# Starting the adjacency gathers beside the loads of x in a two-layer graph attention kernel

## The chip, the cores and the metric

One Trainium2 chip, one core. The metric is the device time of one execution in microseconds (us), as the median of several runs. A profile, taken by the hardware profiler on one execution, gives the times of single instructions and transfers, counted from the start of its span.

## What is computed

Two graph attention layers with residuals on 8192 nodes of 128 features; the adjacency is an 8192 x 8192 int32 matrix, 268 MB, and both layers read it.

```python
h = relu(layernorm(x)); x = x + L0(h, adj)      # L0: attention, threshold 1e-4, times row degree, elu
h = relu(layernorm(x)); x = x + L1(h, adj)      # L1: attention
# in each layer
h = input @ W
e = leaky_relu((h @ a_src)[:, None] + (h @ a_dst)[None, :], 0.2)
att = softmax(where(adj > 0, e, NEG), axis=1)
out = att @ h
```

## The kernel before

The kernel replaces the softmax by a form in which a weight is a maximum of two products, one factor for the row and one for the column, times the adjacency's 0 or 1. For each layer `sum_tiles` runs over 8 groups of 1024 rows and in each over 64 tiles of 128 columns: VectorE forms a weight tile of 128 x 1024 (L906), TensorE multiplies it with h in eight matmuls of 128 x 129 (L659). That is 16384 matmuls in all.

The adjacency comes in by pieces. `load_piece` (GpSimd, L328) gathers 128 rows of 1024 int32 by an indirect DMA, with the row numbers from the tile `piece_rows`; `mask_piece` (ScalarE, L337) turns one into bytes; `turn_edges` (VectorE, L355) transposes the bytes of eight tiles at a time. A pass has 32 pieces (`PIECES`); there are 31 passes, 992 pieces. There are six buffers for pieces (`NA`): gather n, from n = 6 on, waits until mask n - 5 is done. The buffers that the gathers write are not those of x.

The work that comes first is the projection of layer 0. x (8192 x 128 f32, 4.2 MB) is loaded in 8 parts (`XP`) of 1024 rows, each by four DMAs of 128 KB with rows of 512 B: two of each part from SP's queue, two from ScalarE's (`load_x`, L398). SP's queue also has the weights of layer 0 ahead of x and those of layer 1 between parts 3 and 4 (L441 to L445). In the DMA views SP's queue is q1, ScalarE's q10, and that of GpSimd's gathers q0.

Every engine has its order written out by hand, and waits on semaphores in that order. On VectorE (L938 to L980): statistics of parts 0 to 3 (L715), their variance, statistics of part 4, `inverse` for the first half, normalising of parts 0 and 1 (L740), statistics of parts 5 to 7, variance of the second half, normalising of parts 2 and 3, the second inverse, and then `keep_h` (L761), `keep_zT` (L756) and normalising in turn, `extreme_values` with `lin` (L791), `diagonals`. On TensorE (L677 to L691): `turn_z` (L621) for part i + 1 ahead of `products` (L632) for part i, then `spread`, then the sums. On ScalarE (L555 to L568): its 16 loads of x, the square root for the first half (`deviation`, L495), then the 32 masks of the first pass, with `keep_first_zT` 0 to 3 (L504) ahead of masks 3, 4, 7 and 8, the second square root ahead of mask 6, and the exponentials of layer 0 (`exps`, L545 to L552) ahead of mask 30.

On GpSimd (`pool_fast`, L367) `ident` and the first row numbers are made (four IOTAs, L379), then all 992 gathers are issued one after the other. Ahead of the first gather GpSimd waits for part 3 of x, which with the parts before it is half of x, and ahead of the fourth gather for part 7, the last. After gather 48 it makes the other row numbers (eight IOTAs).

Of the kernel before, what the change touches and what calls it, by code (L numbers as in the profile page):

```python
# [44 lines left out]
XP = 8  # L45
# [9 lines left out]
BK = 4  # L55
# [25 lines left out]
def kernel_program(nc, x, adj, W0, a0, W1, a1, out):  # L81
# [10 lines left out]
    def sem(name):  # L92
        if name not in sems:
            sems[name] = ctx.enter_context(nc.semaphore(name))
        return sems[name]

    with ctx:
# [107 lines left out]
        x_loaded = [sem(p + f"x_loaded{i}") for i in range(XP)]  # L205
# [122 lines left out]
        def load_piece(pool, n):  # L328
            g, c, h, k, a = piece(n)
            if n >= NA:  # L330
                pool.wait_ge(masked, n - NA + 1)
            column = ((g * G + 2 * k + h) * BK + a) * COLS + c
            pool.indirect_dma_start(adj_in[n % NA], None, adj_pieces,  # L333
                                    bass.IndirectOffsetOnAxis(ap=piece_rows[:, column:column + 1], axis=0))\
                .then_inc(adj_in_loaded[n % NA], 16)
# [31 lines left out]
        def pool_fast(pool):  # L367
            steps = [0]

            def step(ins):  # L370
                steps[0] += 1
                ins.then_inc(index_made, 1)
                pool.wait_ge(index_made, steps[0])

            def indices(c, t0, t1):
                for b in range(BK):
                    q = slice(b * BP, (b + 1) * BP)
                    tt = slice((c * CT + t0) * BK * COLS, (c * CT + t1) * BK * COLS)
                    step(nc.gpsimd.iota(piece_rows[q, tt].rearrange("p (t a c) -> p t a c", a=BK, c=COLS),  # L379
                                        pattern=[[BP * (N // LC), t1 - t0], [N // LC * LC, BK], [BK, COLS]],  # L380
                                        base=b + (c * CT * P + t0 * BP) * (N // LC), channel_multiplier=N // LC))

            nc.gpsimd.memset(ident[:], 0.0).then_inc(ident_made, 1)
            pool.wait_ge(ident_made, 1)
            nc.gpsimd.affine_select(out=ident[:], in_=ident[:], compare_op=ALU.not_equal, fill=1.0,
                                    base=0, pattern=[[-1, P]], channel_multiplier=1).then_inc(ident_made, 1)
            pool.wait_ge(ident_made, 2)
            indices(0, 0, G)
            pool.wait_ge(x_loaded[XP // 2 - 1], 16 * BK)
            for n in range(len(PASSES) * PIECES):  # L390
                load_piece(pool, n)
                if n == 2:
                    pool.wait_ge(x_loaded[XP - 1], 16 * BK)
                if n == PIECES + PIECES // 2:
                    indices(0, G, CT)
                    indices(1, 0, CT)
# [636 lines left out]
        def fast_program():  # L1033
            with nc.Block() as block:
                @block.sync
                def _(sp):
                    sync_fast(sp)

                @block.scalar
                def _(act):  # L1040
                    scalar_fast(act)

                @block.tensor
                def _(pe):
                    tensor_fast(pe)

                @block.vector
                def _(dve):
                    vector_fast(dve)

                @block.gpsimd
                def _(pool):
                    pool_fast(pool)
# [645 lines left out]
```

## Time and profile before

| | |
|---|---|
| median of 3 runs | 2001.0 us (1999.59 to 2002.02) |
| profiled execution | 2002.71 us, of which its span is 2000.9 us |
| TensorE busy | 1914.1 us, 96% of the span |
| VectorE, ScalarE, GpSimd busy | 87%, 73%, 63% |
| HBM read and written | 548.54 MB and 16.32 MB |

The profiled execution lies 1.7 us above the median. Times inside it are from the start of the span. An engine's busy time says how much it works, not whether it is late; for that, read the chain of work that ended last, and the waits.

### The profile page before, as it was taken

How to read it: one execution, taken by the hardware profiler on the slowest of the kernel's cores; microseconds unless marked ns; L12 is line 12 of the kernel's file. 1: busy time of each engine (PE TensorE's matmuls, PEld its weight loads, DVE VectorE, ACT ScalarE, POOL GpSimd, SP SyncE). 2: the span in 40 equal slices, each digit the busy share in tenths (PEclk: the TensorE clock that was granted, in tenths of full speed). 3: DMA queues.
4: the chain of work that ended last, by engine and by line, in shares of the span. 5: the costliest groups of instructions: out<-in, count | busy, mean ns of one | idle time of the engine just before them, and what ended most of it. 6: DMA issues, size and time to landing. Idle time of an engine off the chain costs nothing.

```text
span 2000.9 us, 39030 instructions
## 1 busy us (share of the span) xinstructions
PE 1914.1 (96%) x16858; PEld 1902.6 (95%) x16858; DVE 1750.4 (87%) x2026; ACT 1453.3 (73%) x1677; POOL 1255.5 (63%) x1010
## 2 busy tenths in 40 slices
PE   4789999999999999999968999999999999999997
PEld 3689999999999999999967999999999999999997
DVE  7888898989989898998957998898989899898985
ACT  4988788969888798888820767777777777778700
POOL 3675766767777676767720556767777776768600
PEclk9799999999999999999988999999999999999999
DMA  8998897999989898897982777888988888889900
GB/s 247 350 339 340 287 334 245 335 335 317 317 287 320 275 321 304 280 320 272 325 283 96 269 295 275 293 311 293 337 276 325 283 296 309 294 315 306 316 10 13
DMA packets 182339, 567.49 MB, mean 284 GB/s; under 512 B 18704, under 2 KB 50832, under 8 KB 180752
## 3 DMA queue, kind: packets, MB, share of 16 engines
q0 software_dynamic: 142848, 520.16, 74.4%
q1 hardware_dynamic: 34960, 42.67, 6.4%
q10 hardware_dynamic: 4352, 2.10, 0.5%
q8 instruction: 133, 2.18, 0.4%
q14 instruction: 46, 0.38, 0.1%
HBM read 548.54 MB, written 16.32 MB: 282 GB/s over the span
## 4 chain that ended last, share of the span: by engine, by line
PE 89%; DVE 6%; DMA 2%; ACT 1%; POOL 1%; issue 0%; SPq 0%; DVEq 0%; POOLq 0%
PE psum L659 87%; PE psum L632 1%; DMA arena<-in_adj_dram,piece_rows 1%; DVE arena L906 1%; DVE arena L740 1%; DVE arena L891 1%; ACT arena L343 1%; DVE arena L884 1%; PE psum L621 0%; DMA arena<-in_x_dram 0%; DVE st L715 0%; POOL piece_rows L379 0%; PE psum L599 0%; DVE arena L361 0%; DVE h_all L761 0%
## 5 line engine op out<-in xcount | busy, mean ns | idle before, releaser
L659 PE MATMUL psum<-h_all,arena 128*128 128x129 f32 x16384 | 1842.4, 276 | 10.4 <-DVE arena L906 10.4
L659 PEld LDWEIGHTS psum<-h_all,arena 128*128 128x128 f32 x16384 | 1837.9, 192 | 14.0 <-DVE arena L906 9.2
L333 POOL DMA_INDIRECT arena<-in_adj_dram,piece_rows x992 | 1246.1, 1256 | 641.4 <-ACT arena L343 446.1
L343 ACT ACTIVATE arena<-arena,half_step 128x1024 uint8<-128x1024 int32 x992 | 1365.1, 1437 | 313.1 <-DVE arena L361 161.3
L906 DVE SCALAR_TENSOR_TENSOR arena<-arena,rho_col 128x1024 f32<-128x1024 f32 x896 | 1125.8, 1277 | 169.1 <-PE psum L659 165.0
L361 DVE STREAM_TRANSPOSE arena<-arena 128x1024 f32<-128x1024 f32 x248 | 305.9, 1234 | 9.1 <-ACT arena L343 9.1
L906 DVE SCALAR_TENSOR_TENSOR arena<-psum,rho_col,arena 128x1024 f32<-128x1024 f32 x128 | 158.7, 1267 | 17.7 <-PE psum L659 14.6
L343 ACT ACTIVATION_READ_ACCUMULATOR arena<-arena,half_step 128x1 f32 x512 | 91.0, 178 | 0.0
L632 PE MATMUL psum<-W_ext,arena 128*128 128x131 f32 x256 | 40.5, 324 | 13.8 <-DVE h_all L761 10.7
L632 PEld LDWEIGHTS psum<-W_ext,arena 128*128 128x128 f32 x256 | 38.1, 234 | 15.4 <-issue 8.1
L621 PE MATMUL psum<-ident,arena 128*128 128x128 f32 x128 | 20.0, 308 | 32.9 <-DVE arena L740 32.5
L621 PEld LDWEIGHTS psum<-ident,arena 128*128 128x128 f32 x128 | 16.9, 160 | 33.9 <-DVE arena L740 33.5
L528 ACT ACTIVATE arena<-arena 128x1024 f32<-128x1024 f32 x8 | 8.5, 1057 | 54.7 <-DVE arena L845 54.7
L740 DVE TENSOR_SCALAR arena<-arena,mean,rstd 128x128 f32<-128x128 f32 x128 | 35.2, 365 | 0.1
L508 ACT ACTIVATE arena<-psum 128x1024 f32<-128x1024 f32 x8 | 8.2, 1024 | 32.3 <-PE psum L621 32.2
L715 DVE BATCH_NORM_STATS2 st<-arena 128x6 f32<-128x128 f32 x128 | 26.0, 277 | 2.5 <-DMA arena<-in_x_dram 2.4
L517 ACT ACTIVATE sd_next<-psum 128x12 f32<-128x12 f32 x16 | 2.9, 181 | 24.7 <-PE psum L632 24.7
L827 DVE TENSOR_TENSOR h_all<-h_all,D_col 128x1024 f32<-128x1024 f32 x16 | 19.4, 1215 | 0.0
L538 ACT ACTIVATE arena<-h_all,invalid 128x128 f32<-128x128 f32 x64 | 19.4, 386 | 0.0
L845 DVE SCALAR_TENSOR_TENSOR arena<-psum,inv,arena 128x128 f32<-128x128 f32 x64 | 17.8, 342 | 0.0
L884 DVE SCALAR_TENSOR_TENSOR arena<-mean_row,fl,arena 128x128 f32<-128x128 f32 x64 | 17.5, 348 | 0.3
L891 DVE SCALAR_TENSOR_TENSOR arena<-psum,inv,arena 128x128 f32<-128x128 f32 x64 | 17.3, 343 | 0.3
(111 smaller groups left out, 180.9 us busy)
## 6 DMA issues: line engine op xcount, KB each, us to landing
arena<-in_adj_dram,piece_rows POOLq DMA_INDIRECT x992, 5.9
arena<-in_x_dram SPq DMA_DIRECT2D x48, 128.0 KB, 6.2
x_mid<-arena SPq DMA_DIRECT2D x8, 512.0 KB, 5.5
edgesT<-arena SPq DMA_DIRECT2D x4, 1024.0 KB, 8.9
arena<-edgesT SPq DMA_DIRECT2D x4, 1024.0 KB, 11.1
arena<-r_mid SPq DMA_DIRECT2D x1, 4096.0 KB, 12.0
arena<-x_mid SPq DMA_DIRECT2D x8, 512.0 KB, 6.8
out_dram<-arena SPq DMA_DIRECT2D x32, 128.0 KB, 9.8
```

Source lines behind the costliest of these rows:

```text
L333: pool.indirect_dma_start(adj_in[n % NA], None, adj_pieces, bass.IndirectOffsetOnAxis(ap=piece_rows[:, column:column + 1], axis=0))\
L343: nc.scalar.activation(pack_bytes[h][:, k, a], adj_in[n % NA], ACT.Sign, bias=half_step[:, 0:1], accum_out=into).then_inc(masked, 1)
L361: nc.vector.transpose(edge_words[:, slot(at), h], pack_words[h][:, s * SBT:(s + 1) * SBT])\
L538: last = nc.scalar.activation(tiles(hr)[:, t, :], h_all[:, b, 0:F], ACT.Identity, scale=D_inv[:, b:b + 1])
L621: last = nc.tensor.transpose(zT_ps(layer, i)[:, t * P:(t + 1) * P], z[:, t, :], ident[:])
L632: last = nc.tensor.matmul(h_ps(layer, i, half)[:, t, :], zT[:, b * P:(b + 1) * P], W_exts[layer][:, 0:HZ], start=True, stop=True)
L659: last = nc.tensor.matmul(acc_tile(g, k), wTs[m % RING][:, k * P:(k + 1) * P], h_all[:, j, 0:FZ], start=(j == 0 and k % 2 == 0), stop=(j = ...
L715: last = nc.vector.bn_stats(st[:, i * TP + t, :], source[:, t, :])
L740: last = nc.vector.tensor_scalar(into[:, t, :], source[:, t, :], mean[:, b:b + 1], rstd[:, b:b + 1], ALU.subtract, ALU.mult)
L884: last = nc.vector.scalar_tensor_tensor(xr[:, cols], mean_row[:], fl[:, k:k + 1], xr[:, cols], ALU.mult, ALU.add)
L891: last = nc.vector.scalar_tensor_tensor(xo[:, cols], acc_tile(g, k)[:, 0:F], inv[:, k:k + 1], xr[:, cols], ALU.mult, ALU.add)
L906: nc.vector.scalar_tensor_tensor(wTs[m % RING].rearrange("p (k n) -> p k n", k=BK), r_of(layer, g), rho_col[:, j:j + 1], edge_bytes[:, slo ...
```

## The change

The two waits of GpSimd for x are taken out. Its gathers are issued as soon as their row numbers stand, six of them, and from the seventh on as each mask frees a buffer.

```diff
             indices(0, 0, G)
-            pool.wait_ge(x_loaded[XP // 2 - 1], 16 * BK)
             for n in range(len(PASSES) * PIECES):
                 load_piece(pool, n)
-                if n == 2:
-                    pool.wait_ge(x_loaded[XP - 1], 16 * BK)
                 if n == PIECES + PIECES // 2:
                     indices(0, G, CT)
                     indices(1, 0, CT)
```

## Rows read from the trace of the kernel before

**Rows 1.** The page, parts 1 and 2: busy us; busy tenths in 40 slices.
```profile
PE 1914.1 (96%) x16858; PEld 1902.6 (95%) x16858; DVE 1750.4 (87%) x2026; ACT 1453.3 (73%) x1677; POOL 1255.5 (63%) x1010
...
PE   4789999999999999999968999999999999999997
```

**Rows 2.** Windows: stretch, its length, busy us (instructions) of each engine, clock, DMA share, GB/s.
```profile
120.00:137.50 17.50, 11.44 (x103) 11.25 (x102) 9.09 (x9) 17.10 (x25) 11.92 (x13) 0.92 1.02 404
137.50:1000.00 862.50, 862.50 (x7707) 862.50 (x7708) 790.05 (x898) 727.78 (x1056) 609.07 (x473) 1.00 0.89 308
```

**Rows 3.** The chain of work, 0 to 160 us: start us, us, what.
```profile
9.15 8.32 DMA arena<-in_x_dram
...
17.50 1.65 DVE st L715 x8
...
37.95 3.85 PE psum L632 x16
...
75.61 0.18 DVE lin L791
...
137.50 22.58 PE psum L659 x183
```

**Rows 4.** Waits of VectorE up to 45 us, of ScalarE up to 80: total, times, longest.
```profile
DVE st L715 <- DMA arena<-in_x_dram: 2.4, 4, 0.7
...
ACT std L495 <- DVE var L725: 5.7, 1, 5.7
...
ACT r_col L545 <- DVE lin L791: 1.3, 1, 1.3
```

**Rows 5.** Timeline: start us, us, engine, line, operation [idle before it and its releaser].
```profile
1.55 1.55 POOL L379 IOTA piece_rows<- 32x64 int32 x4
...
14.78 1.12 POOL L333 DMA_INDIRECT arena<-in_adj_dram,piece_rows  x1 [11.67 <-DMA arena<-in_x_dram]
...
16.20 0.94 POOL L333 DMA_INDIRECT arena<-in_adj_dram,piece_rows  x1 [0.30 <-issue]
...
22.50 0.94 POOL L333 DMA_INDIRECT arena<-in_adj_dram,piece_rows  x1 [4.11 <-DMA arena<-in_x_dram]
...
23.39 1.45 ACT L343 ACTIVATE arena<-arena,half_step 128x1024 uint8<-128x1024 int32 x1 [6.35 <-DMA arena<-in_adj_dram,piece_rows]
...
43.09 1.02 ACT L504 ACTIVATE arena<-psum 128x1024 f32<-128x1024 f32 x1 [4.26 <-PE psum L621]
...
45.56 1.95 PE L632 MATMUL psum<-W_ext,arena 128*128 128x131 f32 x16
```

**Rows 6.** DMA, 5 to 12 us (packets, MB, share of 16 engines); windows, 12 to 19.
```profile
DMA packets 3988, 1.93 MB, mean 275 GB/s; under 512 B 229, under 2 KB 3988, under 8 KB 3988
...
12.00:19.00 7.00, 0.00 (x0) 0.00 (x0) 5.65 (x31) 0.23 (x1) 3.00 (x3) 1.00 1.25 220
```

**Rows 7.** DMA, 22 to 24.5 us.
```profile
q0 software_dynamic: 269, 0.98, 102.6%
```

**Rows 8.** DMA, 96 to 103 us.
```profile
q0 software_dynamic: 599, 2.16, 85.3%
q1 hardware_dynamic: 661, 0.35, 17.5%
```

**Rows 9.** Landing of the loads L427 (80 to 100 us), and of L400 (0 to 10).
```profile
DMA to landing us min/median/max: 11.8/15.0/16.4
...
DMA to landing us min/median/max: 3.0/6.2/9.5
```

**Rows 10.** Landing of the first gather, issued at 14.78 us.
```profile
DMA to landing us min/median/max: 8.6/8.6/8.6
```

**Rows 11.** DMA, 18 to 22 us.
```profile
q1 hardware_dynamic: 726, 0.35, 60.1%
q0 software_dynamic: 142, 0.54, 53.0%
```

**Rows 12.** Windows, as in rows 2.
```profile
38.00:39.00 1.00, 1.00 (x5) 1.00 (x6) 0.42 (x1) 0.83 (x2) 0.00 (x0) 0.50 0.59 86
```

## The prediction

> **What bounds the kernel now.** I read the page first. TensorE is busy for 1914.1 of 2000.9 us, VectorE for 87% of the span, ScalarE for 73%, GpSimd for 63% [rows 1]; in the slices TensorE's digit is 9 all the way except in the first four and at the layer boundary. So the end is set by when TensorE's long run starts. The windows say when that is: from 137.50 to 1000 us TensorE is busy for 862.50 of 862.50 us, and between 120 and 137.5 it works 11.44 us of 17.5 [rows 2]. Whatever moves the restart at 137.5 us moves the end one for one; whatever lies ahead of it and doesn't move it costs nothing.
>
> Then I followed the chain of work back from that restart. It goes through transfers of the adjacency, the mask on ScalarE, an IOTA on GpSimd, to masks that stand behind the exponentials, and these behind VectorE's `lin` at 75.61 us. From there back it is VectorE (statistics, normalising, keeping h) with products on TensorE between, to the statistics at 17.50 us, and these are released by a load of x issued at 9.15 us that took 8.32 us [rows 3]. What isn't in the chain ahead of `lin` is to be seen too: no gather and no mask. The start is a chain of x.
>
> The waits up to 80 us say how near the others are. VectorE waits four times for x, 2.4 us in all. ScalarE waits 5.7 us for the variance and 1.3 us for `lin` [rows 4], 6.35 us for its first gather and 4.26 us for TensorE's fourth transpose [rows 5]. So ScalarE is never the late one ahead of the exponentials.
>
> **What the change removes.** GpSimd's two waits. The first gather is issued at 14.78 us after 11.67 us of waiting for x, the fourth at 22.50 us after 4.11 us [rows 5]. The four IOTAs end at 1.55 + 1.55 = 3.10 us, so the first gather now goes out at about 3.4 us. Issues are 1.24 us apart (16.20 to 17.45), so six of them, as many as there are buffers, are issued by 3.4 + 6 x 1.24 = 10.8 us. The seventh waits for the first mask, as before. No instruction is added; the number of gathers is unchanged.
>
> **What that gives.** The first mask ran at 23.39 us. Now it is held by the code ahead of it on ScalarE, the square root at 16.81 us, so it could run at 17.1 us: 6.3 us earlier. But the eighth mask is followed by `keep_first_zT(3)`, which waits for TensorE's transpose, which waits for VectorE; it ran at 43.09 us after 4.26 us of idling [rows 5]. Masks that are earlier only lengthen that idling. Gain: 0. Behind 43.09 us nothing is different, since six buffers are full then in either kernel; and even there ScalarE had 1.3 us left before `lin`. Bounds: 0 and 0.
>
> **What it costs.** Gathers now share the 16 DMA engines with x. A piece is 128 x 1024 int32, 0.524 MB; six are 3.15 MB. With x alone (5 to 12 us) the two queues move 3988 packets in 7 us, 570 per us, of 512 B: 275 GB/s with the engines busy throughout, about 1.0 MB on each queue [rows 6]. So x has no idle engines to give away. Gathers alone (22 to 24.5 us) move 0.98 MB in 2.5 us, 392 GB/s [rows 7]. When both have work (96 to 103 us, the loads of `load_xr`, of 512 B rows too, beside gathers) the gather queue has 599 packets and SP's queue 661: one for one by packets, which by bytes is 2.16 MB against 0.35 [rows 8]. Those four loads took 11.8 to 16.4 us to land, x at the start 3.0 to 9.5 [rows 9].
>
> Now the sum. 661 small packets at 570 per us are 1.2 us, so 599 gather packets cost 5.8 us, 103 per us. The six gathers need 599 x 3.15 / 2.16 = 873 packets. With three queues in turn a round costs 1/103 + 2/570 us, 75 rounds per us: 11.6 us until the gathers are through, in which x gets 1746 packets, worth 3.1 us of its own time. x falls behind by 8.5 us. From bytes, 3.15 MB at 392 GB/s, it is 8.0 us. I take 7.5 us, since with x alone the rate sagged to 220 GB/s over 12 to 19 us [rows 6], in which a gather finds some room.
>
> Is all of it ahead of the load that counts? That is part 4 of x: issued at 9.15 us, in use at 17.50. Before, no gather had been issued until part 3 had landed. The first gather landed 8.6 us after its issue [rows 10], of which its own 0.524 MB take 1.3 us at 392 GB/s, so a first packet may lag its issue by anything up to 7.3 us. From 3.4 us that is 3.4 to 10.7 us, and 11.6 us later, at 15 to 22 us, the six are done. Part 4 would land near 25 us, behind them in either case. Part 3 is late by nearly the same.
>
> What is late next: VectorE's statistics at 17.50 us go to 25, and with them the inverse, the normalising, every `keep_h`, `lin`, the exponentials, masks 30 and up, and the restart. On VectorE all is in order behind the wait; TensorE and ScalarE wait for VectorE. The slack on the way: 0.7 us ahead of the statistics, but that is itself a wait for x, so none. Parts 5 to 7 are wanted only after parts 0 and 1 are normalised, and have 8 us of x's stream behind part 4 to come in; they cost nothing more. Nothing between 17.5 and 137.5 us in the chain starts by a time of its own, so the delay is passed on whole. Bounds of the cost: 0 (the gathers find no turn before x is through) and 14.6 us. The latter goes by 18 to 22 us, when the mix had 0.35 + 0.54 MB in 4 us, 222 GB/s [rows 11]: with x's share as in rows 8, 3.15 MB of gathers carry 0.51 MB of x along, 3.66 MB are 16.5 us, less 1.9 us that x's part takes alone. I stay by rows 8, since there both queues have work for all of 7 us, at 2.51 MB or 359 GB/s, while 18 to 22 us holds the gathers' first packets only.
>
> The Trainium skill, page "DMA: Bandwidth & Descriptors", section "Queues, rings and completion order", has each engine take one packet from each queue that has work, in turn; by that gathers get their turn as soon as they are there, which speaks against the change and against rival 1. Rows 8 agree, rows 11 at first sight don't. The same page, "Specifications", puts the limit from HBM at about 358 GB/s for a core; rows 7 show 392, so the measurement decides; by the page's figure the six gathers would cost 8.8 us in place of 8.0.
>
> **Forecast.** Sum against the profiled execution: 2002.7 (span 2000.9 and 1.8 around it) + 7.5 = 2010.2 us. The median of the runs, 2001.0, lies 1.7 under that execution, so I predict 2001.0 + 7.5 = 2008.5 us.
>
> **Rival 1: x goes first anyway, no change.** In the row of 18 to 22 us, SP's queue moved 726 packets and the gathers 142, though the first gather had been issued at 14.78 [rows 11]. If gathers get in only as x drains, part 4 lands at 17.5 to 18.5 us and the delay is 0 to 1 us: 2001.5 us. For it: the 8.6 us landing. Against it: one for one in rows 8, and that the end of x's queue is what 18 to 22 us shows. A partial form (gathers start late, three of six ahead of part 4) gives 3 to 4 us: 2004.5. Chance of a delay under 4 us, both forms: 0.25.
>
> **Rival 2: faster, by TensorE's clock.** Three groups of 16 products lie in the chain ahead of `lin`, the first at 37.95 us with 3.85 us [rows 3], while the same 16 take 1.95 us at 45.56 us [rows 5]; the clock granted at 38 us was 0.50, 1.2 GHz [rows 12]. Masks that come earlier let ScalarE do `keep_first_zT(0)` as soon as TensorE has turned part 0, ahead of when it did, and with it TensorE's first products, which shifts TensorE's activity. If x isn't late and all three groups come into stretches at 2.4 GHz, 3 x 1.9 = 5.7 us go: 1995.3 us. It decides the sign only if x is late by less than 5.7 us. Against it: VectorE sets when these groups start, and the pauses between them stay. Chance of faster: 0.08.
>
> **Rival 3: the mix is worse than steady.** If small and large packets together hold the engines to rates between those of rows 8 and rows 11, x is 9.5 to 14.6 us late; the middle gives 2001.0 + 12 = 2013.0 us. For it: the start has three queues at once, rows 8 only two. Against it: rows 8 ran at 359 GB/s for 7 us. Chance 0.12.
>
> **Numbers.** What 3 to 5 runs can tell from no change is about 0.2%, 4 us. Forecast with its near cases (4 to 9.5 us late) 0.55, rival 3 0.12: slower 0.67. Delay or gain under 4 us: 0.25. Faster 0.08. The range takes in rival 1 and the nearer half of rival 3, 2000.5 to 2012.5; the forecast's own is 2005.5 to 2010.5.
>
> **What would show it.** GpSimd's first gather at 3.4 us with no wait for x. VectorE's statistics of part 4 at about 25 us instead of 17.50, and its waits for x near 10 us in place of 2.4. In the DMA rows of 8 to 16 us three queues with nearly equal packets, about 75 per us each. First mask at about 24.5 us, held by the square root. `keep_first_zT(3)` at about 50.5 us. `lin` at 83 us and TensorE's restart at 145 us. The prediction is wrong if the statistics of part 4 stay near 17.5 us, or if they are late but the restart isn't: then ScalarE's masks, not x, had carried the chain.

## The result, and the profile after

The changed kernel takes 2007.33 us (median of 8 runs, 2005.78 to 2011.16) against 2000.39 us (8 runs, 1996.10 to 2002.59): a ratio of 1.0041, 95% interval 1.0029 to 1.0053, so 6 to 11 us slower (6.9 by the two medians). Forecast were 2008.5 us and 7.5 us more. The profiled execution has a span of 2009.3 us, 8.4 us over that of before.

The timeline of the changed kernel, start us, us, engine, line, operation, with the idle time before it and its releaser; its answers to [rows 5] and to the statistics of x's parts 1 to 4:

```profile
3.38 1.12 POOL L333 DMA_INDIRECT arena<-in_adj_dram,piece_rows  x1 [0.28 <-POOL piece_rows L379]
...
9.77 0.93 POOL L333 DMA_INDIRECT arena<-in_adj_dram,piece_rows  x1 [0.30 <-issue]
10.47 12.57 SPq L397 DMA_DIRECT2D arena<-in_x_dram  x8
11.89 1.65 DVE L712 BATCH_NORM_STATS2 st<-arena 128x6 f32<-128x128 f32 x8 [2.52 <-DMA arena<-in_x_dram]
17.61 1.65 DVE L712 BATCH_NORM_STATS2 st<-arena 128x6 f32<-128x128 f32 x8 [4.07 <-DMA arena<-in_x_dram]
...
22.52 1.65 DVE L712 BATCH_NORM_STATS2 st<-arena 128x6 f32<-128x128 f32 x8 [3.27 <-DMA arena<-in_x_dram]
...
25.57 1.65 DVE L712 BATCH_NORM_STATS2 st<-arena 128x6 f32<-128x128 f32 x8 [0.15 <-DMA arena<-in_x_dram]
25.58 1.42 ACT L343 ACTIVATE arena<-arena,half_step 128x1024 uint8<-128x1024 int32 x1
...
51.46 1.02 ACT L501 ACTIVATE arena<-psum 128x1024 f32<-128x1024 f32 x1 [4.79 <-PE psum L618]
```

The gathers go out at 3.38 to 9.77 us with no wait for x. VectorE waits for every part of x that comes beside them, and begins part 4 at 25.57 us in place of 17.50. The first mask isn't 6 us earlier but 2 us later (25.58 for 23.39): it stands behind the square root, and that behind x. The wait ahead of `keep_first_zT(3)` is still there, 4.79 us for 4.26.

The chain of work of the changed kernel, the answer to [rows 3], and one window, the answer to [rows 2]:

```profile
12.22 13.32 DMA arena<-in_x_dram
...
25.57 1.65 DVE st L712 x8
...
46.31 3.84 PE psum L629 x16
...
83.80 0.18 DVE lin L788
...
145.43 24.59 PE psum L656 x199
```

```profile
145.43:1000.00 854.57, 854.57 (x7634) 854.57 (x7635) 782.03 (x886) 719.80 (x1050) 592.43 (x469) 1.00 0.88 308
```

Read down the two chains: 8.07 us late at part 4, 8.36 at the products on TensorE, 8.19 at `lin`, 7.93 at the restart, 8.4 at the end. It is the same chain link by link, begun later. Its first link, a load of x in flight, has grown from 8.32 to 13.32 us, and it begins 3.07 us later (12.22 for 9.15 us), since SP takes longer over the issues ahead of it. So of the 8.07 us at part 4, 5.00 are in flight and 3.07 ahead of the issue.

VectorE's waits up to 55 us, the answer to [rows 4], and DMA packets in the changed kernel by queue over 8 to 14 and 14 to 20 us (packets, MB, share of 16 engines):

```profile
DVE st L712 <- DMA arena<-in_x_dram: 10.2, 5, 4.1
```

```profile
q0 software_dynamic: 395, 1.47, 72.3%
q1 hardware_dynamic: 566, 0.27, 17.5%
q10 hardware_dynamic: 526, 0.25, 15.6%
...
q0 software_dynamic: 450, 1.62, 72.6%
q1 hardware_dynamic: 582, 0.28, 17.1%
q10 hardware_dynamic: 576, 0.28, 16.3%
```

By packets each of x's queues has 1.3 to 1.4 times what the gathers have; by bytes the gathers have three quarters. x had 1.93 MB in 7 us before [rows 6]; here both its queues together have 1.08 MB in 12 us. At 8 us ten gather packets had moved, and behind 20 us nine more, so nearly all of the six gathers went by in these 12 us.

### The profile page after: what moved, and what is told of

It is laid out like the page before. It is cut to its first block, busy times and chain, and to the rows that moved or that the text cites. A ratio compares the mean times of both kernels' runs of the same rounds, so it can differ in the third digit from the quotient of the medians.

```text
span 2009.3 us, 39029 instructions
## 1 busy us (share of the span) xinstructions
PE 1914.0 (95%) x16858; PEld 1902.8 (95%) x16858; DVE 1750.0 (87%) x2026; ACT 1454.0 (72%) x1677; POOL 1249.0 (62%) x1010
## 4 chain that ended last, share of the span: by engine, by line
PE 89%; DVE 6%; DMA 2%; ACT 1%; POOL 1%; SPq 1%; issue 0%; DVEq 0%; POOLq 0%
PE psum L656 87%; PE psum L629 1%; DMA arena<-in_adj_dram,piece_rows 1%; DVE arena L903 1%; ACT arena L343 1%; DVE arena L888 1%; DVE arena L737 1%; DVE arena L881 1%; DMA arena<-in_x_dram 1%; PE psum L618 1%; DVE st L712 0%; POOL piece_rows L379 0%; PE psum L596 0%; SPq L397 0%; DVE arena L361 0%
## 5 line engine op out<-in xcount | busy, mean ns | idle before, releaser
L842 DVE SCALAR_TENSOR_TENSOR arena<-psum,inv,arena 128x128 f32<-128x128 f32 x64 | 17.8, 342 | 0.0
```

## The experiments

Theory A: gathers take time of the DMA engines from x, and what reaches the engines ahead of x's part 4 delays everything. Its rivals, in the expectations: any gather beside x is passed on (B), any work in GpSimd's queue costs the same (C), the number of descriptors counts and not their size (D), masks carry the chain (E), gathers' bytes delay x in whatever packets (F). Diffs are against the kernel before, where nothing else is said. The twelve kernels ran in three groups of four, each beside new runs of the kernel before (median 1999.69 us in the first group, 1998.84 in the third). The ratios are those on record with their intervals, and not quotients of the medians, from which they differ by up to 0.0007.

**Which wait pays.** The wait for all of x is taken out, the one for half of x stays.

```diff
             for n in range(len(PASSES) * PIECES):
                 load_piece(pool, n)
-                if n == 2:
-                    pool.wait_ge(x_loaded[XP - 1], 16 * BK)
```

> The wait for half of x is kept, the wait for all of x ahead of the fourth gather is left out. Theory A (gathers take DMA engine time from x, and only what reaches the engines ahead of x's part 4 counts): the first gather goes out at 14.8 us, its first packet near 19, so part 4 is in by 17.5 us as in the kernel before; parts 5 to 7 are late by the three further gathers, up to 4 us, against a slack of about 6 us on VectorE. Statistics of part 4 at 17.5 us, restart of TensorE at 137.5 us, time 2000 to 2001 us, ratio 1.000. Rival B (any gather beside x is passed on to the end, also through parts 5 to 7): 4 us later, ratio 1.002.

Measured: 2000.72 us, ratio 1.0003 (0.9992 to 1.0015). Rival B falls: its 1.002 is outside. Its timeline has all six gathers issued between 14.54 and 20.94 us, the last three of them 4 us earlier than before, and VectorE is not held:

```profile
14.54 1.12 POOL L333 DMA_INDIRECT arena<-in_adj_dram,piece_rows  x1 [11.44 <-DMA arena<-in_x_dram]
...
16.70 1.64 DVE L713 BATCH_NORM_STATS2 st<-arena 128x6 f32<-128x128 f32 x8 [0.16 <-DMA arena<-in_x_dram]
...
20.94 0.94 POOL L333 DMA_INDIRECT arena<-in_adj_dram,piece_rows  x1 [0.30 <-issue]
...
25.26 4.73 DVE L713 BATCH_NORM_STATS2 st<-arena 128x6 f32<-128x128 f32 x24
```

Part 4 is there at 16.70 us and parts 5 to 7 have no wait at 25.26. With the first wait kept, the second is worth nothing. With the first gone it is worth about half of the loss, as the next runs show: it then holds three of the six gathers back.

**How much for how many.** First three gathers early, then one.

```diff
             indices(0, 0, G)
-            pool.wait_ge(x_loaded[XP // 2 - 1], 16 * BK)
             for n in range(len(PASSES) * PIECES):
                 load_piece(pool, n)
                 if n == 2:
                     pool.wait_ge(x_loaded[XP - 1], 16 * BK)
```

> Only the wait for half of x is left out; the wait for all of x ahead of the fourth gather stays, so three gathers (1.57 MB) run beside x. Theory A: half the cost of the changed kernel, 1.57 MB at 392 GB/s = 4.0 us: statistics of part 4 at 21.5 us, restart at 141.5 us, time 2004.4 us, ratio 1.002. Rival C (what costs is that GpSimd's queue has any work ahead of x, say by filling rings, whatever its amount): the full 8 us, ratio 1.004.

```diff
             indices(0, 0, G)
-            pool.wait_ge(x_loaded[XP // 2 - 1], 16 * BK)
             for n in range(len(PASSES) * PIECES):
                 load_piece(pool, n)
+                if n == 0:
+                    pool.wait_ge(x_loaded[XP // 2 - 1], 16 * BK)
                 if n == 2:
```

> One gather goes out at 3.4 us, the next two wait for half of x and the rest for all of x. Theory A: 0.52 MB at 392 GB/s = 1.3 us: statistics of part 4 at 18.8 us, restart at 138.8 us, time 2001.7 us, ratio 1.0007. Rival C: the full 8 us.

Measured: with three, 2004.88 us, ratio 1.0022 (1.0012 to 1.0032); with one, 2002.84 us, 1.0009 (1.0000 to 1.0019). Part 4 in the two timelines, three and one:

```profile
21.92 1.64 DVE L714 BATCH_NORM_STATS2 st<-arena 128x6 f32<-128x128 f32 x8 [0.38 <-DMA arena<-in_x_dram]
```

```profile
18.60 1.65 DVE L716 BATCH_NORM_STATS2 st<-arena 128x6 f32<-128x128 f32 x8
```

| gathers ahead of part 4 | part 4 begins, us | later than before | ratio | TensorE's restart, us (foretold) |
|---|---|---|---|---|
| 0 (before) | 17.50 | | 1 | 137.50 |
| 1 | 18.60 | 1.10 | 1.0009 | 136.72 (138.8) |
| 3 | 21.92 | 4.42 | 1.0022 | 139.75 (141.5) |
| 6 (the change) | 25.57 | 8.07 | 1.0041 | 145.43 (145) |

That is 1.1 to 1.5 us per gather; 0.524 MB at 392 GB/s are 1.34. The cost goes by the amount, so rival C falls.

The restarts with one and three gathers missed what was expected. With one early gather it came 0.78 us earlier than before, with three 2.25 us later in place of 4. TensorE's longest stretch at 1.2 GHz between 64 and 96 us was 20 us long before and after the change, but 14 us in the execution with three and 7 us in that with one. In the latter the chain of work also leaves VectorE at 44.5 us and goes on through ScalarE's masks to the exponentials, and `lin` is only 0.44 us later than before. That the delay reaches the end is shown here by the medians of 12 runs, and for one gather only just.

**Bytes or descriptors.** Six more gathers, of rows an eighth as long, go out at 3.4 us; nobody uses what they bring, and GpSimd waits for them beside half of x.

```diff
+            small = adj.rearrange("r (w n) -> (r w) n", n=P)
+            for i in range(NA):
+                pool.indirect_dma_start(adj_in[i][:, 0:P], None, small,
+                                        bass.IndirectOffsetOnAxis(ap=piece_rows[:, i:i + 1], axis=0))\
+                    .then_inc(small_loaded, 16)
             pool.wait_ge(x_loaded[XP // 2 - 1], 16 * BK)
+            pool.wait_ge(small_loaded, 16 * NA)
```

> The kernel before, with six more gathers of 128 rows of 512 B (in place of 4096 B) ahead of its first wait, which nobody uses; they are in the same number as the early gathers of the change, with as many descriptors, and an eighth of the bytes. GpSimd waits for them together with half of x. Theory A (engine time by bytes): 6 x 128 = 768 packets at 570 per us are 1.3 us: statistics of part 4 at 18.8 us, ratio 1.0007. Rival D (the number of descriptors or turns, or GpSimd's issuing of them, holds x up, whatever their size): 8 us, statistics of part 4 at 25.5 us, ratio 1.004.

Measured: 2000.58 us, ratio 1.0003 (0.9993 to 1.0013). In its timeline the last of them is issued as in the changed kernel, part 4 is 0.35 us late, and GpSimd's own gathers begin at 17.45 us in place of 14.78, behind its second wait:

```profile
9.82 0.94 POOL L392 DMA_INDIRECT arena<-in_adj_dram,piece_rows  x1 [0.30 <-issue]
...
17.85 1.65 DVE L722 BATCH_NORM_STATS2 st<-arena 128x6 f32<-128x128 f32 x8 [0.69 <-DMA arena<-in_x_dram]
```

The same number of gathers, issued at the same times, with an eighth of the bytes costs next to nothing, less than the 1.3 us of theory A. Rival D falls as far as it means the number of gathers or GpSimd's issuing. It doesn't fall by this run as far as it means packets. DMA over 3 to 18 us:

```profile
DMA packets 8127, 3.96 MB, mean 264 GB/s; under 512 B 1070, under 2 KB 8031, under 8 KB 8127
...
q0 software_dynamic: 192, 0.39, 9.8%
```

The small gathers' 0.39 MB went by in 96 packets of 4096 B (8127 less 8031), beside 96 short ones, and not in 768 of 512 B. So the packets became fewer along with the bytes: 192, where the change has 864. Against a cost by the number of packets speak rows of the changed kernel. At x's 570 packets per us 864 would take 1.5 us, and 8 were lost. Over 14 to 20 us 450 gather packets took 72.6% of the engines' time and 582 of x's took 17.1%, so that one held an engine about 5.5 times as long as the other.

**The second four.** These ran on a chip on which the kernel before took 2220.62 us in place of 2000. Their ratios, in the order below, are 1.0095 (1.0047 to 1.0144), 1.0009 (0.9961 to 1.0057), 1.0100 (1.0029 to 1.0172) and 1.0106 (1.0030 to 1.0181). They don't follow x: the third kernel is 1% slower, though its part 4 is earlier (17.01 us, against 17.50 in the kernel before on the first chip). The first, third and fourth lie above what was expected, and why stays open. Only the first 30 us of the profiles are read here; where the kernel was run again, part 4 began within 0.3 us of the same time (17.17 and 17.11 us, 16.34 and 16.08).

The first gather waits for all of x; then layer 1's weights behind x; then x in rows of 4096 B, without and with the change:

```diff
-            pool.wait_ge(x_loaded[XP // 2 - 1], 16 * BK)
+            pool.wait_ge(x_loaded[XP - 1], 16 * BK)
             for n in range(len(PASSES) * PIECES):
                 load_piece(pool, n)
-                if n == 2:
-                    pool.wait_ge(x_loaded[XP - 1], 16 * BK)
```

> The opposite of the change: the first gather waits for all of x (22.5 us in place of 14.8), so nothing runs beside x. It tests the other half of the argument, that ScalarE's early masks have slack. Theory A: the first mask moves from 23.4 to about 27.5 us. The wait ahead of keep_first_zT(3) (4.3 us) takes most of it, but the second square root, ahead of mask 6, comes about 4 us late, at 37.9 us, and VectorE wants it at 35.8: 2 us late there, time 2002 to 2003 us, ratio 1.001; x's part 4 stays at 17.5 us or comes a little earlier. Rival E (masks carry the chain): 4 us and more, ratio 1.002.

```diff
             for i in range(XP):
                 load_x(sp, i, 0)
-                if i == 3:
-                    load_weights(1, W1, a1)
+            load_weights(1, W1, a1)
```

> The kernel before, with the three loads of layer 1's weights moved on SP's queue from between parts 3 and 4 of x to behind part 7. They have 256 packets of 4 B and 128 of 512 B on the queue that part 4 uses. Theory A (x's part 4 carries the start): part 4 lands about 1.5 us sooner, the statistics of part 4 start at 16.8 us right behind the variance in place of 17.5, and the gain is 0.7 us or less: ratio 0.9997 to 1.000, not to be told by the time. If the weights come late for TensorE (wanted at about 23.5 us) that is lost again.

```diff
+        def long_quarters(ap, i):
+            c, u = divmod(i, XP // COLS)
+            four = ap.rearrange("(c b u j t) f -> c b u j t f", c=COLS, b=BK, u=XP // COLS, j=BP)
+            return [(slice(b * BP, (b + 1) * BP), four[c, b, u]) for b in range(BK)]
...
-            for q, block in quarters(x, i)[2 * which:2 * which + 2]:
+            for q, block in long_quarters(x, i)[2 * which:2 * which + 2]:
```

> The kernel before, with x loaded as rows of 4096 B (each partition takes eight neighbouring rows of x) in place of eight rows of 512 B: the same bytes, an eighth of the packets; x's rows go to other partitions than the rest of the kernel takes them for. Theory A: x alone moves near 390 GB/s in place of 275, parts 3 and 4 land earlier, VectorE's statistics run back to back from about 7 us and part 4's are through at about 16 us: 2 to 3 us gained, 1998 us, ratio 0.999.

> The changed kernel with x in rows of 4096 B, as in the run with long rows. Theory A says that the change costs 8 us because in one round of three queues x moves 2 x 512 B beside 4096 B of gather. With rows of one size x has two thirds of the bytes: 2.6 MB up to part 4 need 3.9 MB in all, 10 us from 2.2 us on and about 2 to land, 14 to 15 us. VectorE, bound by its own statistics, is through with part 4 at 17 us or before: the change costs 0 to 2 us here against the kernel with long rows, ratio to the kernel before 0.999 to 1.000. Rival F (gathers' bytes delay x by themselves, in whatever packets): 6 to 8 us against the kernel with long rows.

Read from them: part 4 began at 17.17 us with all of x first, at 16.34 with the weights last, at 17.01 with long rows (14 to 16 had been expected) and at 26.71 with long rows and the change, which nothing had foretold. For the last, here are the packets by queue over 14 to 20 us:

```profile
q0 software_dynamic: 250, 0.90, 58.0%
q10 hardware_dynamic: 230, 0.62, 40.8%
q1 hardware_dynamic: 245, 0.06, 7.3%
```

SP's queue moved 245 packets but 0.06 MB. Between parts 3 and 4 it has layer 1's weights, whose two vectors are 128 packets of 4 B each. By these counts such a packet takes a turn like any other, while the two other queues move up to 4096 B in theirs. The four were run again, the two with long rows now with the weights behind part 7; part 4 then began at 14.61 us in place of 17.01, and at 19.23 in place of 26.71.

**The third four.** All of x first:

> The opposite of the change once more: the first gather waits for all of x. Theory A: first mask at about 26.7 us, second square root at 37.5 and VectorE's second inverse at 37.8 us in place of 35.8; 2 us late from there, ratio 1.001. Rival E (masks carry the chain): 4 us and more, ratio 1.002.

Measured: 2002.34 us, ratio 1.0013 (1.0004 to 1.0022). VectorE's second inverse is 2.15 us later than before (35.84), released by the square root, as expected; but TensorE's products, 3.83 us long before, are short in this execution:

```profile
37.99 0.35 DVE L728 RECIPROCAL rstd<-std 128x32 f32<-128x32 f32 x1 [2.34 <-ACT std L493]
...
40.16 2.02 PE L630 MATMUL psum<-W_ext,arena 128*128 128x131 f32 x16 [1.77 <-DVE h_all L759]
```

The granted clock over 35 to 45 us was 1.00, against 0.66 in the kernel before. TensorE's first products came later there (32.86 us for 28.58), and with less time ahead of the second (3.4 us for 5.6); I take that for the reason, but no run shows it alone. It more than made the loss of 2 us good in the profiled execution (`lin` 2.1 us earlier than before), and not in the median. The ratio is nearer to A's 1.001 than to rival E's 1.002, whose value the interval reaches. The wait for the square root has the size that A gave it. But the chain of work of this execution doesn't go through VectorE:

```profile
22.36 1.12 POOL arena L333
...
44.11 30.22 ACT arena L343 x44
74.33 0.15 ACT r_col L543
```

It goes from the first gather through ScalarE's masks to the exponentials, which ScalarE reached 0.8 us behind `lin`. So with all of x first the masks did carry the chain in this execution, as rival E says, though not at its price; E isn't excluded by this run. Gathers can be issued too late as well, but 7.6 us later (22.36 us) cost only 2.6 us by the ratio (0.8 to 4.4).

Weights of layer 1 last:

> The kernel before with layer 1's weights behind part 7 of x, once more. Theory A: statistics of part 4 at 16.3 to 16.8 us in place of 17.5, the second inverse about 1 us earlier than 35.8, ratio 0.9995, not to be told from 1 by the time.

Measured: 2000.74 us, ratio 1.0008 (0.9999 to 1.0018). The trace went a little further than foretold, with part 4 at 16.08 us, the second inverse at 34.36 and `lin` at 74.15, 1.5 us earlier than before; the time didn't follow. Inconclusive, and no gain.

Long rows with the weights last, without and with the change. x's rows go to other partitions than the rest takes them for.

> The kernel before with x in rows of 4096 B and layer 1's weights behind part 7, so that their 4 B packets don't take turns ahead of part 4; x's rows go to other partitions than the rest of the kernel takes them for. x alone came at 288 GB/s in rows of 4096 B; statistics of part 4 at about 14 us, right behind part 3's. VectorE's second half is bound by its own order from there: up to 3 us gained, ratio 0.9985 to 0.9995.

> The same with the change (both waits out). Theory A (each queue gets its turn by packets, and a gather packet costs eight x packets' time): with packets of one size x keeps two thirds of the bytes, 35 to 40 packets per us on each queue, about 280 GB/s for x beside 140 for the gathers. Statistics of part 4 at 16 to 18 us, 2 to 3 us later than with long rows and waits, in place of the 8 us that the change costs with rows of 512 B; ratio 1.000 to 1.0005, 0.001 over that of the run with the waits. Rival F (3.15 MB of gathers delay x by 8 us in whatever packets): statistics of part 4 at 22 us, ratio 1.003.

Measured: with the waits 1998.15 us, ratio 0.9994 (0.9985 to 1.0003); with the change 2008.90 us, 1.0046 (1.0033 to 1.0060). Here theory A's figure failed: the change costs 10.8 us in place of 2 to 3. First the packets by queue over 8 to 14 us, without and with the change:

```profile
q1 hardware_dynamic: 340, 0.93, 52.4%
q10 hardware_dynamic: 334, 0.92, 52.0%
```

```profile
q0 software_dynamic: 206, 0.78, 46.1%
q1 hardware_dynamic: 176, 0.48, 29.0%
q10 hardware_dynamic: 174, 0.47, 27.8%
```

The turns hold: 206, 176, 174. But I had taken it that the gathers would come on top of x; the total was 1.85 MB in 6 us without them and 1.73 with them. x falls to half its rate. Part 4 in the two timelines, without and with the change:

```profile
14.61 1.64 DVE L719 BATCH_NORM_STATS2 st<-arena 128x6 f32<-128x128 f32 x8
```

```profile
19.23 1.64 DVE L716 BATCH_NORM_STATS2 st<-arena 128x6 f32<-128x128 f32 x8
```

It is 4.6 us late, between A's 2 to 3 and rival F's 8, though by 17 us only 1.12 MB of the gathers had moved, which at 392 GB/s are 2.9 us. It doesn't wait itself; it stands behind parts 2 and 3, for which VectorE waited 1.64 and 1.52 us. The rest is a new wait. From the timeline with the change:

```profile
20.80 0.34 DVE L731 RECIPROCAL rstd<-std 128x32 f32<-128x32 f32 x1
24.45 1.97 PE L622 MATMUL psum<-ident,arena 128*128 128x128 f32 x8 [16.82 <-DVE arena L741]
...
31.08 0.47 PE L608 MATMUL psum<-ident,W_ext 128*128 128x128 f32 x1 [4.66 <-DMA a_three<-in_L_gnn_a_dram]
...
32.64 4.72 DVE L716 BATCH_NORM_STATS2 st<-arena 128x6 f32<-128x128 f32 x24
```

The weights of layer 1 are now last in SP's queue, behind x and among the gathers, and come 4.66 us after TensorE wants them; VectorE, which waits for TensorE's turn of them, has its statistics of parts 5 to 7 at 32.64 us, 9.7 later than with the waits (22.90). 4.6 + 4.7 is most of the 10.8; `lin` is 9.5 us later, the restart 10.0.

## Why the prediction was right

**What bounds the kernel.** Right, and the experiments widen it. Span less TensorE's restart is 1863.4 us before, 1863.9 after, and between 1862.5 and 1864.0 in the other kernels of the first and third groups, while the restarts lie anywhere from 133.20 to 145.43 us. Nothing behind the restart gives a delay back. (TensorE's digits below 9 are in the first three slices, at the boundary and in the last, not in the first four.)

**What the change removes and gives.** The first gather was foretold for 3.4 us (3.38) and the gain of earlier masks at 0. That the masks would be earlier, had x been in time, was not tried by itself. With the second wait alone taken out the first mask ran 1 us earlier (22.42 for 23.39), but part 4 was 0.8 us earlier too. The kernel with all of x first shows the other side, that later masks cost less than their delay, but also that ScalarE's slack is small: there its masks, 3.5 us late at the first, stood in the chain.

**What it costs.** I took 7.5 us from 8.5 (packets) and 8.0 (bytes), less something for the sag of x's rate; part 4 was 8.07 us late. So 3.15 MB at 392 GB/s was the figure, and the deduction of 0.5 us had no ground. The row that it was taken from says so itself: over 12 to 19 us the DMA share is 1.25, as full as the engines get, and 491 of the 3489 packets were under 512 B. With layer 1's weights last the same stretch has 258 GB/s in place of 220. Foretold were 75 rounds per us for 11.6 us; 66 and then 75 gather packets per us came (395 and 450 in 6 us each), for 12 us. x's queues had up to 97 per us each, 1.3 to 1.4 for one, more than the 1.1 of [rows 8]. The prediction had the load that counts issued at 9.15 us as before. That 3.07 of the 8.07 us would come ahead of its issue was not foreseen; the sum holds all the same, since it counts how far x as a whole falls behind.

**Passed on whole.** Right between the profiles of before and after, with 7.93 us at the restart; `lin` came at 83.80 us and the restart at 145.43, where 83 and 145 had been foretold. It isn't so in those with one and three early gathers. One thing lies over it that I gave as a rival's only. From `lin` to the restart the kernels take between 59.7 and 63.1 us, and between 64 and 96 us TensorE's granted clock is 0.50, 1.2 GHz, for 7 us at a stretch in some executions, 14 in others and 20 before and after. The runs of one kernel lie 4 to 10 us apart, and the mean granted clock goes with it: of the 35 runs of the kernel before in the first group, the 14 at 0.980 to 0.982 have a median of 2001.69 us, the 13 at 0.986 and above one of 1996.91. That the profiles of before and after have the same pattern is luck, and it is why their chains can be laid over each other so well; one profile each wouldn't have told 2 us.

**The rivals.** x goes first: wrong, since gathers had their turn from about 8 us on. The row that spoke for it, 142 gather packets against 726 at 18 to 22 us, showed the last of x's queue and the gathers' first packets, which moved only behind 19.0 us, 4.3 us after the first issue; in the changed kernel it was behind 7.2 us, 3.9 after. The Trainium skill ("DMA: Bandwidth & Descriptors", "Queues, rings and completion order") has each engine serve its queues in turn, a packet at a time. The counts of the three queues agree roughly: 450, 582 and 576 with short rows, 206, 176 and 174 with long ones. Faster by TensorE's clock: with all of x first one group of products took 2.02 us in place of 3.83, but the change didn't bring that about (3.83 at 46.31 us). A mix worse than steady: not here; the rates over 8 to 20 us were 333 and 363 GB/s. It came with long rows, where the mix had 289.

**What stays open.** Why x in rows of 4096 B moves at 309 GB/s alone and no more beside gathers, while gathers alone move 392 with packets of the same size; the experiments give the rates and not the cause. And how much of the 8 us goes through the 4 B packets: the changed kernel too has layer 1's weights ahead of part 4 on SP's queue, without the change they cost part 4 1.4 us (17.50 for 16.08), and the change wasn't run with them last and x in rows of 512 B.

## What to carry to other kernels

A wait that holds a bulk transfer back can be worth its place, even on an engine that has nothing else to do: ask whose bytes would be beside it, and how long the packets are. A queue with rows of 512 B beside one with 4096 B got 1.3 times the packets and about a sixth of the bytes here (0.28 MB for 1.62), so each early gather cost the stream its own whole time on the engines. Ask also what the early data would wait for: here the masks stood behind work that needs x, so starting them earlier could not pay.

## What was unexpected on the chip

- SP's eight issues of x's second half took 12.57 us in the changed kernel, 6.03 before, and ScalarE's sixteen 16.96 in place of 8.86: beside the gathers, the engine that issues x's loads is held too. On SP this stands in the chain: the load of part 4 that counts went out 3.07 us later. ScalarE was free at 17.75 us, still ahead of the square root at 25.45; with less slack this would have been a cost there as well.
- Transfers of 4 B take a turn each. In the first run with long rows and the change, 245 packets with 0.06 MB went by in 6 us on the queue that part 4 stood in, and part 4 began at 26.71 us.
- The prediction named part 4 as the load that counts. VectorE's waits lie ahead of it, on parts 1 to 3 (2.52, 4.07 and 3.27 us, and 0.15 on part 4), since every part comes late in turn.
- Gathers of 512 B rows showed as packets of 4096 B (96 for 0.39 MB), while x's loads with rows of 512 B from SP and ScalarE showed as packets of 512 B. A row's length in the code is not the packet's: look it up in the DMA view.
